# Edge stage of a graph network: the pair counts between the sums of the two ways

## The reference

```
agg  = segment_sum(mlp([x[src], x[dst], e]), dst)      # way 0
agg += segment_sum(mlp([x[dst], x[src], e]), src)      # way 1
x    = layernorm(x + three gated recurrent cells on x and agg)
x    = layernorm(x + gin(x))       # three layers: (1+eps) X + A X, then a two-layer mlp
```

## Time and profile before

| | |
|---|---|
| median of three runs | 2393.22 us (2392.76 to 2396.28) |
| the profiled execution | 2392.77 us, span 2391.0 us |
| TensorE matmul busy | 2270.7 us, 95% |
| VectorE busy | 1759.5 us, 74% |
| ScalarE busy | 1230.0 us, 51% |
| GpSimd busy | 1146.1 us, 48% |
| granted TensorE clock, mean | 0.984 |

### The profile page before, as it was taken

One profiled execution on the slowest core, in us unless ns is written; L12 is line 12 of the kernel. 1 busy time (PEld: TensorE's weight loads), 2 busy tenths in 40 slices (PEclk: granted clock), 3 DMA queues, 4 the chain that ended last, 5 costly groups with the idle time before them and its releaser, 6 DMA issues. The chain is left out here.

```text
span 2391.0 us, 39551 instructions
## 1 busy us (share of the span) xinstructions
PE 2270.7 (95%) x12547; PEld 1874.5 (78%) x12547; DVE 1759.5 (74%) x4056; ACT 1230.0 (51%) x2106; POOL 1146.1 (48%) x846
## 2 busy tenths in 40 slices
PE   4999999999999999999999999999999879799996
PEld 3888888888888888888888888888888645588785
DVE  8888888888888888888888888888888557502114
ACT  4566566566556565566666565665665313211112
POOL 2556666566566566565665665665666300000000
PEclk9999999999999999999999999999999879899998
DMA  5355445445445444554454454454545550395873
GB/s 162 74 122 123 98 89 109 89 90 107 97 96 104 87 105 94 95 110 91 87 110 89 97 111 87 96 104 86 110 99 94 60 218 1 134 390 225 327 294 137
DMA packets 233138, 292.58 MB, mean 122 GB/s; under 512 B 126815, under 2 KB 190661, under 8 KB 224599
## 3 DMA queue, kind: packets, MB, share of 16 engines
q1 hardware_dynamic: 159556, 237.05, 32.3%
q0 software_dynamic: 73216, 54.58, 17.6%
q10 hardware_dynamic: 272, 0.05, 0.0%
HBM read 218.51 MB, written 73.08 MB: 122 GB/s over the span
## 5 line engine op out<-in xcount | busy, mean ns | idle before, releaser
L473 POOL DMA_INDIRECT sums<-outb,target x416 | 669.0, 1608 | 609.7 <-ACT outb L643 443.1
L466 POOL DMA_INDIRECT xg<-in_x,gidx x416 | 472.3, 1135 | 158.9 <-issue 140.3
L1240 PEld LDWEIGHTS ebank<-w3t,h 128*128 128x128 f32 x3328 | 387.4, 192 | 8.3 <-issue 0.3
L1240 PE MATMUL ebank<-w3t,h 128*128 128x128 f32 x3328 | 388.2, 275 | 0.2 <-ACT h L625 0.2
L1228 PE MATMUL ebank<-h1h,w2h 128*128 128x512 f32 x832 | 363.8, 437 | 3.4 <-DVE h1l L852 3.3
L625 ACT ACTIVATE h<-ebank,b2c 128x512 f32<-128x512 f32 x416 | 286.3, 688 | 119.8 <-issue 100.4
L611 ACT ACTIVATE h1h<-hpre 128x512 fp32r<-128x512 f32 x416 | 257.9, 628 | 150.8 <-DVE hpre L848 114.1
L1228 PE MATMUL ebank<-h1h,w2l 128*128 128x512 f32 x832 | 328.2, 394 | 0.0
L1228 PE MATMUL ebank<-h1l,w2h 128*128 128x512 f32 x832 | 325.9, 392 | 0.0
L852 DVE SCALAR_TENSOR_TENSOR h1l<-hpre,h1h 128x512 fp32r<-128x512 f32 x416 | 270.6, 690 | 17.3 <-ACT h1h L611 14.4
L848 DVE TENSOR_TENSOR hpre<-pb,ebank 128x512 f32<-128x512 f32 x416 | 265.1, 677 | 2.5 <-PE ebank L1214 2.3
(11 more groups left out here) (266 smaller groups left out, 3791.7 us busy)
## 6 DMA issues: line engine op xcount, KB each, us to landing
ring<-adj SPq DMA_DIRECT2D x54, 1568.0 KB, 8.2
rowb<-along SPq DMA_DIRECT2D x104, 512.0 KB
ef<-in_edge_attr SPq DMA_DIRECT2D x103, 256.0 KB
adj<-band SPq DMA_DIRECT2D x48, 480.0 KB
adj<-band SPq DMA_DIRECT2D x24, 540.0 KB
stay<-adj SPq DMA_DIRECT2D x6, 1568.0 KB, 14.4
xg<-in_x,gidx POOLq DMA_INDIRECT x416
sums<-outb,target POOLq DMA_INDIRECT x416
```

Source lines behind the costliest of these rows:

```text
L466: pool.indirect_dma_start(out=to, out_offset=None, in_=a["x"], in_offset=bass.IndirectOffsetOnAxis(ap=ids, axis=0)).then_inc(s_x[par], 16)
L473: pool.indirect_dma_start(out=tables[k % 2], out_offset=bass.IndirectOffsetOnAxis(ap=target[par][:, 1, k:k + 1], axis=0), in_=outb[par][:, ...
L1240: last = nc.tensor.matmul(bank[6 + way][:, t * P:(t + 1) * P], h2[:, way, k, t * P:(t + 1) * P], w3t[:, k, :], start=not bias and k == 0, ...
```

## The change

On TensorE `pairs_of(g)` leaves its place between `turn_sd` and `second(g,1)`. `pairs_of(g + 1)` now stands in `total(g)`, behind the first sum and ahead of the wait for the second `es` copy, and gets a wait for the last `hpre` of its group, as it writes the banks that `hpre` is computed from. On VectorE the turn goes: first count, `nodes` of the next group, second count, `compare`, `sums`, and only then `places`. Group 0 keeps its order. Nothing is added to or left out of the computation.

```diff
 def turn(g, par, turns, ahead=2, early=0, fresh=None, wrapped=None):      # VectorE
     begin = isinstance(g, int) and g == 0
-    if ahead:
-        nodes(g + 1, 1 - par, early=early == 2)
-        compare(g + 1, 1 - par, turns + par)
-    places(g, par, early=early > 0)
-    if ahead:
-        sums(g + 1)
     if begin:
+        nodes(1, 1, early=True)
+        compare(1, 1, 0)
+        places(0, 0, early=True)
+        sums(1)
         pair_keys()
         pair_hot(0)
         lower_parts(1)
         dve.wait_ge(s_band, 2)
         dve.wait_ge(s_ztab, 2 * 16)
-    if fresh is not None:
-        dve.wait_ge(s_fresh, fresh)
-    count_pairs(g, 0)
-    count_pairs(g, 1)
+        count_pairs(0, 0)
+        count_pairs(0, 1)
+    else:
+        if fresh is not None:
+            dve.wait_ge(s_fresh, fresh)
+        count_pairs(g, 0)
+        if ahead:
+            nodes(g + 1, 1 - par)
+        count_pairs(g, 1)
+        if ahead:
+            compare(g + 1, 1 - par, turns + par)
+            sums(g + 1)
+        places(g, par, early=early > 0)
     if ahead and not begin:
         lower_parts(g + 1)
...
 def pairs_of(g):                                                          # TensorE
     pe.wait_ge(s_ah, g + 1)
+    pe.wait_ge(s_hp, g * 4 + 4)
...
-def total(g, par):
+def total(g, par, ahead):
...
     last.then_inc(s_sum, 1)
+    if ahead:
+        pairs_of(g + 1)
     pe.wait_ge(s_es, g * 2 + 2)
...
     if begin:
         pair_keys()
-    else:
-        pairs_of(g)
     second(g, 1)
...
-    total(g, par)
+    total(g, par, ahead)
```

## The result

The changed kernel takes 2399.5 us (median of 15 runs, 2395.2 to 2407.5) beside 2393.3 us (15 runs, 2391.8 to 2396.9) of the kernel before on the same chip: ratio 1.0021, interval 1.0013 to 1.0029. That is a small loss where the prediction had a gain of 10 us; 2399.5 lies inside the range but close to its upper end. On another chip, with five rounds, the ratio was 1.0062 (1.0042 to 1.0082).

What follows compares the result with a forecast made beforehand. TensorE was taken to bound the edge loop. Terms of -18.3 us (es waits), +6.6 (h waits) and +1.5 (wraps) summed to -10.2 us, from 2392.8 to 2383 us, with a range of 2363 to 2401.

Steps and rivals of the forecast that it cites:

- (1): TensorE: the pair counts leave their place behind L1258, where they cost 0.96 us a group.
- (2): TensorE: pair counts between the two sums move L1293 0.85 us later and cover the es waits, -18.3 us.
- The rule weighed there: TensorE's queue pulls weight loads ahead of running matmuls: each place worth 0.85 us, time some 10 us lower.
- (3): The added s_hp wait costs nothing; the second sum 0.85 us later is nothing to the gather/scatter engine.
- (4): VectorE's counts: the first's exposed register load (0.73 us) and the hidden nodes (0.34) about balance.
- (5): VectorE's sums of rows wait for TensorE's product of L1258 and run 0.56 us late.
- (6): TensorE's second(g,3) waits for ScalarE's second h, 0.07 us in each of 95 groups, +6.6 us.
- (7): VectorE's later sdl leaves L1214 0.04 us of room, costing nothing; the eight wraps cost +1.5 us.
- A: Rival: the h wait of (6) does not bind, 95 groups gain 0.11 us each, 2366 us; chance 0.13.
- B: Rival, no change: sdl holds L1214 back by a further 0.1 us, +9.5 us, 2392 us; chance 0.17.
- C: Rival, slower: the register load behind the late pair counts becomes VectorE's path, 2402 or 2421 us; chance 0.10.
- D: Rival, slower: whatever makes the copy late hits sd or the upper halves; 18.3 us return, 2401 us; chance 0.06.

Runs made afterwards that it cites:

- e8: Changed kernel with SyncE's bulk loads (ef, rowb, xw) held back until after second(g,2): ratio 0.9944, 2385.0 us.
- e7: Kernel before the change with SyncE's loads of ef and rowb held back in the same way: ratio 1.0006.
- e5: Changed kernel with one wait more, GpSimd starting the gathers only when outb is there: 2431.1 us, ratio 1.0139.
- e10: Kernel before the change with the gathers from the third group on replaced by a semaphore count: 2374.0 us, ratio 0.9902.
- e4: Changed kernel with the gathers from the third group on replaced by a semaphore count: ratio 1.0053.

## Why the prediction was wrong, step by step

**(1), (2) the place of the pair counts: right in kind.** The second product of L1228 came 1.42 us after L1258; now it comes 0.65 after L1265, 0.77 less, not 0.96. At the new place they cost 0.85. The idle weight load of 0.36 did not move with them: the earlier trace rows have it at L1272, after has it at L1235, behind L1265. It belongs to what follows the one-hot products. TensorE gained 0.04 in the group instead of 0.11. The rule weighed there had the price at the new place right, 0.85, was 0.08 too high at the old one (0.77), and says nothing of the idle load that stayed.

**(2) the waits for `es`: right.** Of the 18.3 us 2.2 are left, so the term is -16.1 us.

**(3) nothing for GpSimd: this is the step that failed.** The prediction weighed 0.85 us of delay against over 4 us of idle time and was right so far. It never asked what the loads of SyncE do, whose event is the transposes of `ef`: against the scatter-adds these moved 0.75 us forward. Nor did it ask whether VectorE's new order touches GpSimd, whose first three scatter-adds of a group now take 2.0, 1.8 and 2.0 us to issue (medians) instead of 1.6 each. The second scatter-add then lands late, the fourth waits for it, and the last gather begins 2.0 us later in the period: at 14.63 us instead of 12.66 (medians). In e8, with the loads held back, it begins at 13.34, so a third of the shift goes with the longer issues and the rest with the loads. The signals that the gathers hold up are then no longer one `es` that the pair counts cover, but those around the sums: of the 90 late ones 25 are L1303's, 24 L1280's, 18 L1296's and 16 L1247's. In place of the nothing that was written there, the transposes wait 17.0 us more than before, and the waits for `h` and at the first layer, which the prediction had elsewhere, 9.4 us more. e8 and e7 show the part of the loads: the same two lines take 1.0062 to 0.9944 in the changed kernel and leave the one before at 1.0006. That comparison of the changed kernel is across two chips of nearly the same time of before; the waits (199.8 to 39.9 us for landings, 36.7 to 15.5 at the transposes) say the same.

**(4) the counts: right.** The second count's load shows 0.39 us behind `nodes`, the sums wait for TensorE, as written.

**(5) the sums of rows: right.** They start 0.51 us later against the first sum; 0.56 was worked out.

**(6) the wait for `h`: a size, 0.07 us a group, that is not there.** `h` ended 8.28 us after the first sum (8.34 worked out), and from its end to the product went 0.18, where 0.23 were taken. In an undisturbed group the term is 0; over the run L1235 waits for `h` 9 times, 5.4 us more than before, and not a little in every group, as the +6.6 us had it.

**(7) `sdl` and the wraps: right but for some ten groups.** `sdl` ends 9.57 us after the first sum (9.65 worked out) and holds nothing there. But about every fifth group the weight load of L1221 begins only 0.13 us after the end of `sdl`, 0.42 to 0.48 us of idle time behind it; over the run that wait has grown by 4.0 us. The wraps cost 1.9 us instead of 1.5.

The rivals: A is refuted as a time, though the condition that it named, no wait for `h`, did hold. B occurred in those ten groups only, C not at all. D is what happened in outline: a copy was late again, at a place where that matters (`outb` and not the `sd` or upper halves that it named). Its 2401 beside 2399.5 is in part luck, as 1.8 us of the loss are the clock's. But it was given 6 in 100, and its mechanism was left as "whatever makes the copy late". That was the mistake: a repeating wait of 0.4 us whose producer had long been done was priced as a gain without asking for its cause. The trace had it: nearly all the late copies follow a product that ended 1.2 us after the start of the group's last gather. Of the signs of being right the mean period failed, 17.78 us where 17.55 to 17.70 were named.

What stays open is why signals are held up while GpSimd issues indirect transfers, why only some of them, and why on one chip none. That a load's traffic is what delays the second scatter-add is shown only by moving the loads together; which of the two, and whether the write-out of the band next to them takes part, was not separated. Nor was it tried what in VectorE's new order lengthens the scatter-adds' issues, and the changed kernel and e8 were never timed on one chip.

## What to carry to other kernels

When instructions are moved on one engine, list every event that they stood ahead of or behind, and for each other queue work out how its issues now lie against each other; here two DMA queues were shifted by 0.75 us against each other although neither was touched. A wait that ends long after its producer is a finding to be explained before it is booked as a gain, because its cause goes on to hit something else. And look at the spots where a stage's rare work (here the wrap) stands in front of a critical chain: moving it a few microseconds later, to where VectorE idles, was worth 11 us, nearly as much as the change once its loads were held back (14 us), while the change by itself lost 6.

## What the runs showed of the hardware

- TensorE's signals can take effect 0.2 to 1.9 us late while GpSimd issues an indirect gather or scatter-add: 54 in the trace of the kernel before, 90 and 116 in two of the changed one, 150 in e5. With gathers left out there were none (e10), and the time is 2374 to 2375 us on both chips that this was tried on. One chip showed none in four traces, two of them with all gathers.
- A weight load stands idle for 0.36 us behind the 64-row one-hot products whatever follows them, bf16 or f32.
- VectorE's f16 to bf16 operations go from 0.24 and 0.33 to about 0.6 us in some of the cases where they run beside a scatter-add's issue (in e4 43 of 307 and 46 of 420).
- The issue of a scatter-add takes 1.6 us with VectorE's order of before and 1.8 to 2.1 us with the new one, in the first three of a group, but 1.6 in e5 and for the first two in e4; the cause is open.
